# Patch attention in a one-core transformer kernel: value-stationary weighing and a new order of the stage

## What is computed

```python
q = einsum('ed,bdw->bew', Wq, qp) + bq[:, None]   # qp: patches of layernorm(x), (32, 128, 128)
k = einsum('ed,bdw->bew', Wk, qp) + bk[:, None]
val = einsum('ed,bdw->bew', Wv, vp) + bv[:, None] # vp: patches of the context
scores = einsum('bhdi,bhdj->bhij', qh, kh) / sqrt(8); scores = where(mask > 0, scores, -1e9)
o = einsum('bhij,bhdj->bhdi', softmax(scores), vh).reshape(32, 64, 128)
out = einsum('de,bew->bdw', Wo, gelu(o)) + bo[:, None]; out = out * masks
```

## Time and profile before

| | us |
|---|---|
| median of three timed runs | 3216.49 (3211.46 to 3218.92) |
| profiled execution | 3217.37 |
| its span | 3215.5 |
| the stage, from the first SP load to the next stage | 995.7 to 1283.4 |
| busy in the whole span: PE, DVE, ACT, POOL | 2912.2, 1977.6, 1362.0, 1328.4 |

### The profile page before, as it was taken

One profiled execution on the slowest core, in us unless ns is written; L12 is line 12 of the kernel. 1 busy time (PEld: TensorE's weight loads), 2 busy tenths in 40 slices (PEclk: granted clock), 3 DMA queues, 4 the chain that ended last, 5 costly groups with the idle time before them and its releaser, 6 DMA issues. The chain is left out here.

```text
span 3215.5 us, 44808 instructions
## 1 busy us (share of the span) xinstructions
PE 2912.2 (91%) x16404; PEld 2526.5 (79%) x16404; DVE 1977.6 (62%) x3545; ACT 1362.0 (42%) x3376; POOL 1328.4 (41%) x1180
## 2 busy tenths in 40 slices
PE   7999999999865778489999998998999999999967
PEld 6888888888753776377888887887999999999955
DVE  5777777777753555767988886335444444444453
ACT  4656556656511443123444443222444434444520
POOL 6555445554313551246555552002443434443430
PEclk9999999999967776699999999999999999999988
DMA  4122112221021000211111112100011101010000
GB/s 130 45 60 65 56 51 60 62 62 49 24 79 41 10 7 1 59 40 47 43 43 40 38 37 90 44 29 27 27 27 27 27 18 30 24 27 21 17 27 26
DMA packets 77816, 131.86 MB, mean 41 GB/s; under 512 B 10016, under 2 KB 23584, under 8 KB 77216
## 3 DMA queue, kind: packets, MB, share of 16 engines
q1 hardware_dynamic: 68096, 112.09, 11.7%
q10 hardware_dynamic: 9504, 16.91, 1.6%
HBM read 114.23 MB, written 14.75 MB: 40 GB/s over the span
## 5 line engine op out<-in xcount | busy, mean ns | idle before, releaser
L89 PE MATMUL a_pa<-a_wo,a_ot 128*128 128x512 f32 x2304 | 538.6, 391 | 10.3 <-issue 7.5
L89 PEld LDWEIGHTS a_pa<-a_wo,a_ot 128*128 128x128 f32 x2304 | 429.6, 188 | 105.9 <-issue 13.0
L359 DVE SCALAR_TENSOR_TENSOR a_nf_acc<-a_nf_t,a_nf_acc 128x512 f32<-128x512 bf16 (+1 forms) x462 | 402.5, 871 | 46.8 <-ACT a_nf_t L313 15.9
L313 ACT ACTIVATE a_nf_t<-a_nf_w,a_nf_shifts 128x512 bf16<-128x512 f32 (+1 forms) x495 | 321.8, 708 | 178.7 <-DVE a_nf_w L343 149.4
L89 PE MATMUL a_pa<-h_t,a_wqk 128*128 128x512 f32 x1536 | 373.7, 396 | 1.7 <-DVE h_t L770 1.7
L89 PEld LDWEIGHTS a_pa<-h_t,a_wqk 128*128 128x128 f32 x1536 | 282.3, 189 | 56.6 <-DVE h_t L770 1.9
L89 PE MATMUL a_pa<-a_wv,ctx_t 128*128 128x512 f32 x960 | 234.3, 403 | 38.6 <-POOL a_wv L1617 23.0
L89 PEld LDWEIGHTS a_pa<-a_wv,ctx_t 128*128 128x128 f32 x960 | 183.7, 194 | 78.2 <-POOL a_wv L1617 24.3
L89 PE MATMUL a_pa<-ctx_t,a_wqk 128*128 128x512 f32 x960 | 224.6, 390 | 1.2 <-POOL a_wqk L1617 1.0
L89 PEld LDWEIGHTS a_pa<-ctx_t,a_wqk 128*128 128x128 f32 x960 | 179.7, 188 | 39.6 <-POOL a_wqk L1617 2.4
L1006 POOL TENSOR_TENSOR a_prob<-a_prob,a_inv 128x512 f32<-128x512 f32 x128 | 130.6, 1042 | 182.5 <-DVE a_inv L1372 182.5
(11 more groups left out here) (358 smaller groups left out, 6188.1 us busy)
## 6 DMA issues: line engine op xcount, KB each, us to landing
a_raw<-in_a_w SPq DMA_DIRECT2D x288, 256.0 KB, 2.6
a_nf_w<-in_nf ACTq DMA_DIRECT2D x32, 256.0 KB, 2.7
nf_rounded<-a_nf_acc ACTq DMA_DIRECT2D x32, 256.0 KB, 2.0
f_rows<-nf_rounded SPq DMA_DIRECT2D x22, 256.0 KB, 2.9
ctx_kept<-ctx_t SPq DMA_DIRECT2D x1, 4096.0 KB, 16.2
ctx_t<-ctx_kept SPq DMA_DIRECT2D x1, 4096.0 KB, 14.3
f_cols<-nf_rounded SPq DMA_DIRECT2D x11, 256.0 KB, 3.8
a_ctx_raw<-in_ctxt SPq DMA_DIRECT2D x4, 512.0 KB, 6.5
```

What stands on the lines that cost most here:

```text
L89: ins = nc.tensor.matmul(out, lhs(a), rhs(b), start=first and i == 0, stop=last and i == 2)
L313: self.nc.scalar.activation(self.t[:, m % NF4_RING, cols], self.w[:, p % 2, cols], ACT.Identity, bias=self.shifts[:, u - 2:u - 1], scale=s ...
L359: ins = nc.vector.scalar_tensor_tensor(acc, t, c, acc, inner, outer)
```

## The change

- The values become the stationary operand. `vp` has 80 columns a head, the 72-column window of head h holds its 8 values at column 8h and a one at 64 + h, with zeros elsewhere; the weights `ep` move, 128 columns a head, and the 8 heads accumulate into one tile of 72 rows x 128 columns. Rows 0 to 63 are the weighed values, already turned, rows 64 to 71 the sums. `pov` has two banks, one per batch parity. `turn_weighed`, `pot` and `o2` go.
- Division per batch: `inverse` takes one reciprocal of 8 rows x 512, a projection "r" spreads it to all rows by a small product with `sel`, ACT copies the 64 rows (`keep_weighed`), DVE multiplies (`divided`).
- PE's order in a round: scores(n + 2), weigh(n), transposes(n + 1), projections. Keys of b + 2 go in round 1, "r" of b - 1 and the first query part in round 2, the second in round 3; outputs of batches 0 to 3 in the last two rounds.
- `hp` and `cp` exist twice; the splits are issued in round 0, normed rows three batches ahead, low context two.
- The start: the norm's power comes before the mask's row, DVE makes the first two low halves and three of the first four key placements, `vp` is cleared by ACT, the mask is loaded behind the first two context tiles, `sel` is one more small load. Projections and first scores are interleaved.
- The end: POOL adds the first six outputs to x. `gone` takes one instruction. Memory is laid out by hand, with `gp` over dead tiles.

```diff
-VC = 10
+VW = DK + PH
+VSTEP = VW + DH
...
-    order = pair("k", 0) + pair("q", 0) + [("v", 0, 0)] + pair("k", 1) + pair("q", 1)
+    order = pair("k", 0) + pair("q", 0) + pair("k", 1) + [("v", 0, 0)] + pair("q", 1)
...
-    return order + [("y", b, 0) for b in range(NB)]
+    return order + [("y", 4, 0), ("r", NB - 1, 0), ("y", 5, 0), ("y", 6, 0), ("y", 7, 0)]
...
-    kind, of = {0: ("v", b + 1), 1: (None, NB), 2: ("k", b + 2), 3: ("q", b + 2)}[s]
...
+    work = {0: [("v", b + 1, 0)], 1: [("k", b + 2, 0), ("k", b + 2, 1)], 2: [("r", b - 1, 0), ("q", b + 2, 0)],
+            3: [("q", b + 2, 1)]}[s]
+    work = [key for key in work if 0 <= key[1] < NB]
+    if b == NB - 1 and s >= 2:
+        work += [("y", 2 * (s - 2) + i, 0) for i in range(2)]
+    return work
...
+    def place_rows(engine, b, i):
+        dst = kd[rows(i), b % 2, :, :, i, :]
+        src = k32[rows(i), :, :].rearrange("p t (s n) -> p t s n", n=P)
+        add = gone[rows(i), None, :].broadcast_to([ROWS, 2, D]).rearrange("p t (s n) -> p t s n", n=P)
+        return engine.tensor_tensor(dst, src, add, ALU.add)
...
-            sp.dma_start(mask[:, :, :].rearrange("p b n -> p (b n)"),
-                         mask_in.rearrange("(o b) n -> o (b n)", o=1).broadcast_to([P, NB * D])).then_inc(mask_loaded, 16)
...
+                if b == 2:
+                    sp.dma_start(mask[:, :, :].rearrange("p b n -> p (b n)"),
+                                 mask_in.rearrange("(o b) n -> o (b n)", o=1).broadcast_to([P, NB * D])).then_inc(mask_loaded, 16)
...
+                    pool.wait_ge(kd_done, placed(b - 1))
+                    pool.wait_ge(kd_first, 3)
+                nc.gpsimd.tensor_scalar(gone[:, :], mask[:, b, :], 0.0, neg_row[:, 0:1], ALU.is_le, ALU.mult).then_inc(gone_set, 1)
...
-                pool.wait_ge(gone_set, b + 1)
-                pool.wait_ge(hp_lo, max(b, 1) + 1)
-                pool.wait_ge(cp_lo, max(b - 1, 0) + 1)
...
+                for i in range(1 if b == 0 else 4):
+                    place_rows(nc.gpsimd, b, i).then_inc(kd_done, 1)
...
+                nc.gpsimd.memset(kd[:, slot, :, :, :, :].bitcast(F32), 0.0).then_inc(kd_zero, 1)
+            norm.rstd_on_gpsimd(nc, pool)
...
+            pool.wait_ge(vp_zero, 1)
+            nc.gpsimd.memset(vp[:, :, :, DK:DK + (PH - 1) * (VW + 1) + 1:VW + 1], 1.0).then_inc(ones_set, 1)
...
             pool.wait_ge(mask_loaded, 16)
             mask_row(0)
-            norm.rstd_on_gpsimd(nc, pool)
-            rest_of_h(0)
-            nc.gpsimd.memset(vp[:, :, :, :, DH:VC], 1.0).then_inc(ones_set, 1)
+            pool.wait_ge(kd_zero, 2)
+            place_keys(0)
             rest_of_ctx(0)
-            rest_of_h(1)
-            pool.wait_ge(kd_zero, 1)
...
+            rest_of_ctx(1)
...
             mask_row(1)
-            pool.wait_ge(kd_zero, 2)
             place_keys(1)
+            rest_of_h(2)
...
+                if s == 1:
+                    if b + 3 < NB:
+                        rest_of_h(b + 3)
+                    if b + 2 < NB:
+                        rest_of_ctx(b + 2)
+                        pool.wait_ge(cp_lo, b + 3)
+                        mask_row(b + 2)
                 if s == 2 and b + 2 < NB:
                     place_keys(b + 2)
+            for b in range(BY_POOL):
+                pool.wait_ge(y_done, b + 1)
+                nc.gpsimd.tensor_tensor(x[:, b, :], x[:, b, :], y[:, b % 2, :], ALU.add).then_inc(x_added, 1)
...
+                elif kind == "r":
+                    pe.wait_ge(rs_done, b + 1)
+                    ins = nc.tensor.matmul(out, sel[DK:VW, :], rs[DK:VW, :], start=True, stop=True)
...
-                    ins = nc.tensor.matmul(pov[:, head * VC:(head + 1) * VC], ep[:, n % 2, head, :], vp[:, b % 2, s, head, :],
-                                           start=True, stop=True)
+                    ins = nc.tensor.matmul(pov[0:VW, b % 2, s * P:(s + 1) * P], vp[:, b % 2, s, head * VW:(head + 1) * VW],
+                                           ep[:, n % 2, head, :], start=head == 0, stop=head == PH - 1)
                 ins.then_inc(pv_ready, 1)
...
-            for key in tiles[:9]:
+            for key in tiles[0:4]:
                 project(key)
             scores(0)
+            for key in tiles[4:6]:
+                project(key)
             scores(1)
+            for key in tiles[6:9]:
+                project(key)
             transposes(0)
             pe.wait_ge(ones_set, 1)
             for n in range(N):
                 if n + 2 < N:
                     scores(n + 2)
+                weigh(n)
                 if n + 1 < N:
                     transposes(n + 1)
-                if n > 0:
-                    turn_weighed(n - 1)
                 for key in patch_work(n):
                     project(key)
-                weigh(n)
-            turn_weighed(N - 1)
-            for b in range(NB):
-                project(("y", b, 0))
+            for key in tiles[-5:]:
+                project(key)
...
+            def keep_weighed(b):
+                act.wait_ge(rs_done, b + 1)
+                nc.scalar.activation(o_all[side(b), b // 2, :], pov[0:DK, b % 2, :], ACT.Copy).then_inc(o_kept, 1)
...
+            nc.scalar.activation(vp[:, :, :, :].rearrange("p b s (c n) -> p (b s c) n", n=P),
+                                 ident[:, None, :].broadcast_to([P, 2 * NP * PH * VSTEP // P, P]), ACT.Copy, scale=0.0
+                                 ).then_inc(vp_zero, 1)
...
+            split_h(0)
+            split_ctx(0)
+            split_h(1)
             act.wait_ge(w_split, 2)
-            split_ctx(0)
-            split_h(0)
             for key in tiles[0:4]:
-                minus_hi(key)
-            split_h(1)
-            for key in tiles[5:9]:
                 minus_hi(key)
             split_ctx(1)
             exp(0)
+            for key in tiles[4:6]:
+                minus_hi(key)
+            split_h(2)
             exp(1)
+            for key in tiles[7:9]:
+                minus_hi(key)
             copy_weights(0)
...
+                if s == 0 and b > 0:
+                    keep_weighed(b - 1)
+                if s == 0 and b + 3 < NB:
+                    split_h(b + 3)
+                if s == 0 and b + 2 < NB:
                     split_ctx(b + 2)
-                if s >= 2:
-                    for key in patch_work(n):
+                for key in patch_work(n):
+                    if key[0] in "kq":
                         minus_hi(key)
...
+            def divided(b):
+                key = ("r", b, 0)
+                dve.wait_ge(pj_ready, made_count[key])
+                dve.wait_ge(o_kept, b + 1)
+                o = o_all[side(b), b // 2, :]
+                nc.vector.tensor_tensor(o, o, bank(key)[side(b), :], ALU.mult).then_inc(pj_used, 1)
+                dve.wait_ge(pj_used, made_count[key])
+                dve.sem_inc(o_done, 1)
...
+                nc.vector.scalar_tensor_tensor(y[:, b % 2, :], bank(key), bo[:, 0:1], mask[:, b, :], ALU.add, ALU.mult
+                                               ).then_inc(pj_used, 1)
+                dve.wait_ge(pj_used, made_count[key])
+                dve.sem_inc(y_done, 1)
+                if b >= BY_POOL:
+                    nc.vector.tensor_tensor(x[:, b, :], x[:, b, :], y[:, b % 2, :], ALU.add).then_inc(x_done, 1)
...
+            def inverse(b):
+                dve.wait_ge(pv_ready, NP * (b + 1))
+                if b > 0:
+                    dve.wait_ge(pj_ready, made_count["r", b - 1, 0])
+                nc.vector.reciprocal(rs[DK:VW, :], pov[DK:VW, b % 2, :]).then_inc(rs_done, 1)
...
             dve.wait_ge(norm.rstd_ready, 1)
             apply(0)
             apply(1)
...
+            for b in range(2):
+                dve.wait_ge(hp_hi, b + 1)
+                nc.vector.tensor_tensor(hp[:, b, LO, :], hn[:, b, :], hp[:, b, HI, :].bitcast(F32), ALU.subtract
+                                        ).then_inc(hp_lo, 1)
+            dve.wait_ge(w_split, 2)
+            apply(2)
+            for key in tiles[0:2]:
                 work(key)
-            apply(2)
+            dve.wait_ge(pj_used, 2)
+            dve.wait_ge(gone_set, 1)
+            dve.wait_ge(kd_zero, 2)
+            for i in range(1, 4):
+                place_rows(nc.vector, 0, i).then_inc(kd_first, 1)
+            for key in tiles[2:4]:
+                work(key)
             shifted(0)
+            dve.wait_ge(kd_first, 3)
+            for key in tiles[4:6]:
+                work(key)
             shifted(1)
+            dve.wait_ge(vp_zero, 1)
+            for key in tiles[6:9]:
+                work(key)
...
-                if n > 0:
-                    divided(n - 1)
                 if n + 2 < N:
                     shifted(n + 2)
-                if s == 0 and 2 < b + 2 < NB:
-                    apply(b + 2)
+                if s == 0 and b > 0:
+                    inverse(b - 1)
+                if s == 0 and b + 3 < NB:
+                    apply(b + 3)
```

(73 more changed lines are left out.)

173 lines of the change are left out of this document (58 added, 115 removed).

## The result

The changed kernel took 3161.57 us in the median of four executions. One of the four was a slow one of 16278.73 us; the other three lie between 3156.91 and 3164.61, with 3158.54 in the middle, and the ratio is taken from them. It is 0.9824 of the kernel before, 95% interval 0.9808 to 0.9839. The profiled execution took 3164.61, with a span of 3162.1. The forecast was 3156, with a range of 3132 to 3187.

What follows compares the result with a forecast made beforehand. Batches were taken as bound by the VectorE-ScalarE loop and the value projection's wait for low context. Savings of 23.8, 36.6 and 1.0 less 0.1 made 61.3, taking 3217.4 to 3156 us; range 3132 to 3187.

Steps and rivals of the forecast that it cites:

- the gap: Before each batch's value projection: TensorE's wait for GpSimd's low context, 4.4 to 6.0 us, claimed to go.
- A: Stage start up to the first weighing, 61.3 us before: claimed 23.8 us less, give or take 5.
- B: Six batches from the first weighing: 22.9 us each instead of 29.0, set by VectorE's loop, 36.6 us less.
- The clock in B: TensorE in the six batches: full clock claimed, its idle splitting into pieces of about 1 us.
- slower rival: Whole stage: granted clock stays at 0.50, a batch takes 37.4 us, total 3268; chance 0.06.
- C: Last two batches, seventh batch's first weighing to the last weighing's end: 35.5 us instead of 36.5, 1 us less.
- the inverse in round 0 some 0.5: Last two batches: the reciprocal in a batch's first round claimed to add some 0.5 us.
- exposed copy: Last two batches: weighing waits for copies of transposes issued just before, some 0.4 us of a 3.75 us round.
- D: Tail, last weighing's end to the last sum into x: 14.9 us instead of 14.8, 0.1 us more.
- A cheap reciprocal: Reciprocal per batch at the plain rate, 0.7 us instead of 3.3: batch 20.3, total 3137; chance 0.12.
- The clock falls in every batch: Six batches: clock still falls, or bank and buffer waits line up badly; about 26 us each, total 3178; chance 0.20.

Runs made afterwards that it cites:

- cols16: Changed kernel with the weighing in nearly the old form, softmax weights stationary and 16 columns moving, values tile filled with ones: 3188.88 us, ratio 0.9915.
- keys_dve: Changed kernel with all four key placements of the first batch on VectorE, GpSimd idle until they are done: 3156.37 us, ratio 0.9813.
- sums_copied: Changed kernel with the reciprocal of the 8 x 512 sums replaced by a plain copy: 3136.82 us, ratio 0.9757.
- gap: Changed kernel with the old due times: low context late, keys and queries bunched in rounds 2 and 3: 3182.5 us, ratio 0.9901.
- gap_cols16: Changed kernel with both the 16-column weighing and the old late due times of context, keys and queries: 3222.5 us, ratio 1.0024.
- again: The changed kernel measured once more, nothing altered: 3160.71 us, ratio 0.9831.

## Why the prediction was right, step by step

That the total came so near is partly luck. The batches were 5.1 us better than forecast, the start, the last two batches and the tail 9.1 worse, and the forecast started from 3217.4, which is 3.0 above the median of the comparison. Luckier still is the clock: it was expected to rise because the gap went. With the gap gone but the form as in `cols16`, the kernel took 3188.88 us, outside the range.

*A, 1.6 us short.* TensorE started at 1008.04 (1009.3 forecast), the mask's row at 1010.30. The three placements on VectorE were costed at 1.23 each from a plain sum, 3.7, and took 6.70:

```profile
1008.04 2.90 PE L89 MATMUL a_pj<-a_hp,a_w 128*128 128x512 f32 x6 [13.78 <-DVE a_hp L2634]
...
1010.30 2.03 POOL L2322 TENSOR_SCALAR a_gone<-a_mask,a_neg_row 128x512 f32<-128x512 f32 x1 [4.60 <-DMA a_mask<-in_mask_f]
...
1020.87 1.19 PE L2403 MATMUL a_psc<-a_kd,a_qp 128*128 128x512 f32 x2 [7.01 <-DVE a_qp L2552]
```

The failed step took a duration from a row in which the other engine was idle. `keys_dve` showed it: 1.24 alone. The placements began at 1012.58, 0.4 to 1.1 us ahead of the forecast, which hid a part of the 3.0; the scores came at 1020.87 instead of about 1019.

*B, 5.1 us better.* The rounds came out at 6.9, 5.7, 5.1 and 5.1, sum 22.8, against 7.1, 5.7, 5.0 and 5.0; the weighing at 1.91 (1.87), "r" at 1.05 from start to start (0.9), the reciprocal at 3.35 (3.3). That VectorE's loop sets the batch is shown by `sums_copied`. The reciprocal had the price of the three old rows' slope, 3.3. The estimate by the Trainium skill (VectorE: DVE Perf Modes, "First, the fixed hardware budget"), with its repeat count of 8 read as eight cycles a column, gave 4.3, and the measurement decides for 3.35. Of the 5.1 us, 3.9 are a slip in the sum: six batches were priced in full, but the first has no reciprocal behind it and took 19.0 (1034.94 to 1053.91). The last took 22.2.

*The clock in B: right in size, its reason incomplete.* The forecast took full clock because the gap of 4.4 goes. `gap` shows that this is the smaller half: with the gap and the new form the clock was 0.84. `cols16` shows the larger: without the gap and nearly in the old form it was 0.63, with TensorE idle for 0.7 us in all. The forecast priced the form by its rate alone (1.87 against 1.70 a round), and at full clock the two do take the same, 1.91 and 1.95. By the clock the form of `cols16` costs some 5 us a batch, 30 in B. That the stage had half rate "with TensorE fully busy" stood in the prediction as an argument of the slower rival; `cols16` brings such stretches back with its form, and the 128-column rows of the other stage were the right evidence against that rival.

*C, 4.6 us too good.* Up to the 30th weighing, at 1190.27, C took 22.9 where 20.8 were forecast, and from there 17.2 instead of 14.7. The failed term of the first part is "the inverse in round 0 some 0.5":

```profile
1172.06 3.35 DVE L2605 RECIPROCAL a_rs<-a_pov 8x512 f32<-8x512 f32 x1
...
1177.94 1.00 PE L2403 MATMUL a_psc<-a_kd,a_qp 128*128 128x512 f32 x2 [2.73 <-DVE a_e L2597]
...
1188.81 3.35 DVE L2605 RECIPROCAL a_rs<-a_pov 8x512 f32<-8x512 f32 x1
...
1192.20 1.29 DVE L2591 TENSOR_REDUCE a_top<-a_psc 128x4 f32<-128x512 f32 x2
...
1202.24 1.65 PE L89 MATMUL a_pj<-a_gp,a_wo 64*128 64x512 f32 x3 [1.85 <-DVE a_o_all L2568]
...
1203.81 3.69 PE L2424 MATMUL a_pov<-a_ep,a_vp 128*72 128x128 f32 x16
```

TensorE waits 2.73 in that round. The second part has a term that the forecast left out: the reciprocal at 1188.81 stands ahead of the last maximum, at 1192.20, and so of the last exponential. With a copy in the reciprocal's place the first part was 2.7 shorter, the second 1.2, and C 36.3, near the forecast 35.5. What is left over in the second part, some 1.4, was not traced. The last weighing at half clock (3.69) was nearly the same before, 3.59. The exposed copy, 0.4 forecast, was 0.46 where it could be read.

*D, 2.9 us too good.*

```profile
1210.52 3.35 DVE L2605 RECIPROCAL a_rs<-a_pov 8x512 f32<-8x512 f32 x1 [0.22 <-PE a_pj L89]
...
1214.02 2.04 PE L2384 MATMUL a_pj<-a_rs,a_sel 8*128 8x512 f32 x2 [3.69 <-DVE a_rs L2605]
...
1218.56 1.26 POOL L2367 TENSOR_TENSOR x<-x,a_y 128x512 f32<-128x512 f32 x1 [2.50 <-DVEq L2580]
1218.57 1.80 DVE L2614 TENSOR_TENSOR a_gp<-a_o_all,a_gp 128x512 fp32r<-128x512 f32 x1
...
1224.56 0.69 DVE L2582 TENSOR_TENSOR x<-x,a_y 128x512 f32<-128x512 f32 x1
```

The reciprocal starts 3.0 after the last weighing's end (2.5 forecast). The "r" product came after an idle of 3.69 at half clock, 2.04 instead of 1.0, and the low half of the gelu took 1.80 instead of 0.7 beside a sum on GpSimd. These three are 2.6 of the 2.9. The forecast had costed "r" at full clock, although by its own sum TensorE stands idle for the reciprocal just before.

*The rivals.* A cheap reciprocal was priced at 18.7 us less; `sums_copied`, with the reciprocal replaced, has a stage 19.3 shorter. That its total of 3136.8 meets the rival's 3137 is partly chance, as some 5 us of it lie outside the stage. "The clock falls in every batch" (3178) and "slower" did not come; `gap_cols16`, with the clock at 0.63 in the batches, is what that side looks like, 3222.5.

## What to carry to other kernels

When an operation moves to another engine or form, take its duration from a row in which the neighbours that it will have were running, and its clock from a row with the same form. Where the clock is low while the engine is busy throughout, as in `cols16`, look for the cause in the instructions and try it by changing their form alone. A long operation per batch belongs, cut up, into the waits that the timeline shows; here two parts of 1.75 us, in place of one of 3.35, gave 18.4 us of the stage. And where the rest of the program scatters by more than the gain, compare the stage and not the total.

## What the hardware showed

- In the two places read here where sums of two SBUF operands on VectorE and GpSimd met, they took turns. The row pair above: VectorE's started 0.01 after GpSimd's of 1.26 and took 1.80, near 1.25 of waiting and its own 0.69. At the start VectorE's three placements took 1.22, 3.25 and 2.17 one after another. The second ended at 1017.08, 1.09 after GpSimd's placement, which in its turn had taken 3.27 instead of 2.40. The Trainium skill (SBUF — State Buffer, "🔬 SBUF: two separate sides") says that the two engines lock a shared port pair for a whole instruction, VectorE with two SBUF inputs against a GpSimd operation that reads SBUF; this case's rows agree, and it would have warned of A's term, had it been weighed.
- VectorE's reciprocal: 3.35 us for 512 columns of 8 partitions, 1.75 for 256, so 6.25 ns a column on 0.15, close to the line of the three short rows (6.2 on 0.154).
- Sixteen weighing instructions take 1.91 with weights of 72 columns and 128 moving, and 1.95 with weights of 128 and 16 moving, at full clock. The form didn't show in their time, only in the granted clock of the stretch (0.99 and 0.63). Nor did the narrower weights show in the loads: in B of `again` one of 72 columns took 146 ns in the mean, and one of 128 columns, for the transposes, 141.
- After the wait of 5.30 us in `gap`, the granted clock was 0.50 from the return of work at 1107.73 to 1114.9. After one of 2.73 the next weighing took 1.91 in the changed kernel and 3.16 in `keys_dve`, where nothing differs in that place.
